# Cross-attention of a decoder layer: half of the probability tiles turned by VectorE in 32x32 squares and placed by DMA through DRAM

## The reference

```
q = (x @ Wq + bq), k = (ctx @ Wk + bk), v = (ctx @ Wv + bv)   split into 16 heads of 64
att = softmax(q * (1 / sqrt(8)) @ k.T)                        512 x 512 per batch and head
out = concat(att @ v) @ Wo + bo
x = layernorm(x + out)
```

## Time and profile before

| | us |
|---|---|
| runs shown, median of 3 (least, most) | 1960.04 (1959.64, 1960.54) |
| profiled execution, its own time | 1960.26 |
| its span, first to last instruction | 1958.4 |
| mean granted TensorE clock, share of full speed | 0.999 |
| cross-attention, roughly | 360 to 1740 |

### The profile page before, as it was taken

The page is one execution under the profiler, slowest core; times in us unless marked ns, Lnnn a source line. Parts: engine busy times, 40 slices in busy tenths (PEclk is TensorE's granted clock), DMA queues, the critical chain, the costliest instruction groups (busy, mean ns, idle before and its releaser), DMA issues.

```text
span 1958.4 us, 29643 instructions
## 1 busy us (share of the span) xinstructions
PE 1941.7 (99%) x9856; PEld 1632.4 (83%) x9856; DVE 1475.2 (75%) x3134; ACT 1149.4 (59%) x2462; POOL 729.5 (37%) x858
## 2 busy tenths in 40 slices
PE   8999999999999999999999999999999999999998
PEld 7888888788888888888888888888888888788887
DVE  5676666787777777777777777777777788867887
ACT  5445544676666666666766666666666667632221
POOL 2322342132343433332333333333333343527763
PEclk9999999999999999999999999999999999999999
DMA  5777778863556536364553726355462636321221
GB/s 215 274 285 280 300 280 318 277 218 106 185 171 189 186 116 195 98 192 140 184 168 101 237 65 215 107 162 172 119 193 66 194 115 218 130 87 44 86 87 65
DMA packets 112086, 334.87 MB, mean 171 GB/s; under 512 B 9152, under 2 KB 9152, under 8 KB 107200
## 3 DMA queue, kind: packets, MB, share of 16 engines
q1 hardware_dynamic: 111936, 332.98, 51.2%
HBM read 211.31 MB, written 88.08 MB: 153 GB/s over the span
## 4 chain that ended last, share of the span: by engine, by line
PE 94%; DVE 2%; ACT 2%; issue 1%; DMA 0%; POOL 0%; ACTq 0%; DVEq 0%; POOLq 0%
PE a_proj L1311 17%; PE a_turned L1311 17%; PE a_score L1324 11%; PE a_av L1348 11%; PE a_proj L48 9%; PE a_proj L1335 5%; PE a_turned L1335 5%; PE a_proj L1739 4%; PE a_av L1739 4%; PE a_score L48 3%; PE a_av L48 3%; ACT c_prob L1019 1%; PE a_score L1714 1%; PE a_turned L1698 1%; PE a_turned L612 1%
## 5 line engine op out<-in xcount | busy, mean ns | idle before, releaser
L958 POOL TENSOR_SCALAR c_prob<-c_prob,all_rden 128x512 f32<-128x512 f32 x512 | 350.2, 698 | 881.8 <-DVE all_rden L1128 881.8
L1019 ACT ACTIVATE c_prob<-a_score,all_negmax 128x512 f32<-128x512 f32 x512 | 348.0, 685 | 211.6 <-DVE all_negmax L1122 208.8
L1122 DVE TENSOR_REDUCE all_negmax<-a_score 128x1 f32<-128x512 f32 x512 | 329.3, 685 | 186.4 <-PE a_score L1324 186.1
L1324 PE MATMUL a_score<-c_ks,c_qs 128*128 128x512 f32 x1024 | 277.6, 391 | 3.3 <-ACT c_prob L1019 3.0
L1348 PE MATMUL a_av<-c_pt,c_vs 128*128 128x512 f32 x1024 | 277.1, 391 | 0.0
L1324 PEld LDWEIGHTS a_score<-c_ks,c_qs 128*128 128x128 f32 x1024 | 190.5, 188 | 44.7 <-ACT c_prob L1019 5.9
L1348 PEld LDWEIGHTS a_av<-c_pt,c_vs 128*128 128x128 f32 x1024 | 192.0, 188 | 39.8
L1168 DVE TENSOR_TENSOR c_pt<-a_proj,c_pt 128x512 fp32r<-128x512 f32 x258 | 171.9, 686 | 27.0 <-ACT c_pt L1047 25.0
L1311 PE MATMUL a_proj<-all_second_buffer,c_wq 128*128 128x512 f32 x756 | 188.0, 397 | 0.0
L1311 PE MATMUL a_turned<-all_third_buffer,all_first_buffer 128*128 128x512 f32 x732 | 182.6, 398 | 0.0
L1168 DVE TENSOR_TENSOR c_pt<-a_turned,c_pt 128x512 fp32r<-128x512 f32 x254 | 169.1, 686 | 9.0 <-ACT c_pt L1047 5.3
(11 more groups left out here) (207 smaller groups left out, 3275.0 us busy)
## 6 DMA issues: line engine op xcount, KB each, us to landing
all_first_buffer<-ctxT_scratch SPq DMA_DIRECT2D x64, 512.0 KB, 7.4
c_wk<-wk_scratch SPq DMA_DIRECT2D x64, 512.0 KB, 3.8
c_wq<-wq_scratch SPq DMA_DIRECT2D x64, 512.0 KB, 6.1
all_second_buffer<-x1T_scratch SPq DMA_DIRECT2D x16, 2048.0 KB, 14.8
c_ks<-c_ks SPq DMA_DIRECT2D x128, 256.0 KB, 5.6
ctxT_scratch<-s_csp SPq DMA_DIRECT2D x8, 2048.0 KB, 7.4
c_y<-y_steps_scratch SPq DMA_DIRECT2D x16, 1024.0 KB, 6.1
y_steps_scratch<-c_y SPq DMA_DIRECT2D x15, 1024.0 KB, 10.0
```

What stands on the lines that cost most here:

```text
L958: nc.gpsimd.tensor_scalar(prob[:, n % 2, i, :], prob[:, n % 2, i, :], rden[:, n % 2, i:i + 1], 1.0, ALU.mult, ALU.mult).then_inc(p_ready, 1)
L1019: nc.scalar.activation(prob[:, n % 2, i, :], spsum[:, i % 2, :], ACT.Exp, bias=negmax[:, n % 2, i:i + 1], scale=1.0, accum_out=den[:, n % ...
L1122: nc.vector.tensor_reduce(negmax[:, n % 2, i:i + 1], spsum[:, i % 2, :], AX.X, ALU.max, negate=True).then_inc(smax, 1)
L1324: ins = nc.tensor.matmul(spsum[:, i % 2, :], qs[:, j % 2, e, i * P:(i + 1) * P], ks[:, j % 2, e, m, :], start=(m == HI), stop=(m == LO))
```

## The change

For all heads but three (the first two and the last, `WHOLE`), TensorE turns only the first two blocks of 128 keys. The other two take another way. VectorE turns `prob[:, n % 2, 256:, i]` (128 x 256) of each of the four query tiles in place, in squares of 32x32 (`flip`); SyncE stores the 128 x 1024 values of the head to DRAM (`store_flips`, 512 KB) and loads them back with four DMAs, each to 32 partitions in pieces of 512 bytes (`load_flips`), to `landing`. ScalarE casts the landed tile to its high part (`flip_hi_tile`), and GpSimd subtracts in place for the low part (`flip_lo_tile`).

So that a piece is 512 bytes long, the four query tiles lie interleaved: `prob` is [128, 2, 512 keys, 4] instead of [128, 2, 4, 512 keys], and exp, normalisation and turning step over 16 bytes; the turnings write their PSUM bank with the same step (`squares`), and `o_second` reads it so and puts the queries back in order.

The order of the work changes with it. `MIDDLE`, `FIRST` and `LAST` are new orders of the items. Values of blocks 0 and 1 come two steps after their turning, those of blocks 2 and 3 in the step 2n + 4 of head n. The context and x are loaded in two pieces per step from ScalarE's queue (`BULK`), as are the V and O weights. SyncE's order is by step (`sync_step`): after the item's weights, a store of flips in an even step, their load in the odd one, then the doubling of K. The wait on the stored y moves to step 13. The tests on GpSimd's and VectorE's passed counters share one semaphore, the ready signals of V and O weights are replaced by TensorE's direct waits, x1T is loaded in four pieces, the feed-forward weights are split two to four steps later and stored by piece, and some buffers move.

```diff
@@ cross_attention
-    TILES, STEPS, LEAD, LAG = T * HH, T * HH // 2, 4, 4
+    TILES, STEPS, LEAD = T * HH, T * HH // 2, 4
+    Q, TURNED, FLIPPED = 32, 2, 2
+    SQUARES = P // Q
...
-    NEXT = ["V0+", "K0+", "Q0+", "V1+", "V2+", "K1+", "Q1+"]
-    MIDDLE = ["V3", "K2", "Q2", "O0", "O1", "O2", "K3", "Q3", "O3"] + NEXT
-    FIRST = ["V2", "V3", "K2", "", "Q2", "", "K3", "", "Q3"]
-    NEXT_TO_FIRST = NEXT
-    LAST = ["V3", "K2", "Q2", "", "O0", "", "K3", "", "Q3", "", "O1", "", "O2", "", "O3", ""]
+    NEXT = ["V0+", "K0+", "Q0+", "V1+", "K1+", "V2+"]
+    MIDDLE = ["Q1", "K2", "Q2", "V3", "O0", "O1", "K3", "Q3", "O2", "O3"] + NEXT
+    FIRST = ["V2", "K2", "Q2", "V3", "", "", "K3", "", "Q3", ""] + NEXT
+    LAST = ["Q1", "K2", "Q2", "V3", "", "O0", "K3", "Q3", "", "O1", "", "O2", "", "O3", "", ""]
...
+    WHOLE = (0, 1, HH * GROUPS - 1)
+    def turned_in(g, step):
+        n, half = divmod(step, 2)
+        return [(g, T * n + k) for k in ((2 * half, 2 * half + 1) if HH * g + n in WHOLE else (half,))]
+    def valued_in(g, step):
+        n, half = divmod(step, 2)
+        tiles = [(n - 1, 1)] if half else [(n - 2, 2), (n - 2, 3), (n - 1, 0)]
+        return [x for x in (tile_of(g, *tile) for tile in tiles) if x]
...
+    def store_flips(g, n):
+        head = HH * g + n
+        sp.wait_ge(flipped, T * FLIPS[head])
+        wait(sp, landed[head % 2], 16 * SQUARES * (LANDINGS[head] - 1))
+        sp.dma_start(flips[head % 2], prob[:, n % 2, TURNED * P:, :].rearrange("p c i -> p (c i)")).then_inc(
+            flip_stored, 16)
+    def load_flips(g, n):
+        head = HH * g + n
+        sp.wait_ge(flip_stored, 16 * FLIPS[head])
+        wait(sp, av_mm, T * (head - 1))
+        src = flips[head % 2].rearrange("(a p) (k c n) -> c p k a n", a=SQUARES, k=FLIPPED, c=SQUARES)
+        dst = as_f32(landing[:, head % 2, :, :]).rearrange("p k (a n) -> p k a n", a=SQUARES)
+        for c in range(SQUARES):
+            sp.dma_start(dst[c * Q:(c + 1) * Q], src[c]).then_inc(landed[head % 2], 16)
...
     def norm_tile(g, t):
-        nc.gpsimd.tensor_scalar(prob[:, n % 2, i, :], prob[:, n % 2, i, :], rden[:, n % 2, i:i + 1], 1.0,
+        nc.gpsimd.tensor_scalar(prob[:, n % 2, :, i], prob[:, n % 2, :, i], rden[:, n % 2, i:i + 1], 1.0,
                                 ALU.mult, ALU.mult).then_inc(p_ready, 1)
+    def flip_lo_tile(g, n, k):
+        head = HH * g + n
+        pool.wait_ge(flip_hi, FLIPPED * (FLIPS[head] - 1) + k + 1)
+        whole = landing[:, head % 2, k, :]
+        nc.gpsimd.tensor_tensor(whole, as_f32(whole), as_f32(flip_hi_part[:, k, :]), ALU.subtract).then_inc(flip_lo, 1)
...
     def pool_group(g):
+            if step == 3 and g:
+                split_out(g - 1, PAIRS - 1)
+            if landed_head(g, step):
+                for k in range(FLIPPED):
+                    flip_lo_tile(*landed_head(g, step), k)
             for tile in ahead(g, step):
                 norm_tile(*tile)
-            if step == 1 and g:
-                split_out(g - 1, PAIRS - 1)
+            if step == 0 and g:
+                split_out(g - 1, PAIRS - 2)
...
     def exp_tile(g, t):
-        nc.scalar.activation(prob[:, n % 2, i, :], spsum[:, i % 2, :], ACT.Exp,
+        nc.scalar.activation(prob[:, n % 2, :, i], spsum[:, i % 2, :], ACT.Exp,
...
+    def flip_hi_tile(g, n, k):
+        head = HH * g + n
+        act.wait_ge(landed[head % 2], 16 * SQUARES * LANDINGS[head])
+        wait(act, av_mm, T * (head - 1) + TURNED + k + 1)
+        nc.scalar.copy(flip_hi_part[:, k, :], as_f32(landing[:, head % 2, k, :])).then_inc(flip_hi, 1)
...
     def scalar_group(g):
+            if landed_head(g, step):
+                for k in range(FLIPPED):
+                    flip_hi_tile(*landed_head(g, step), k)
+            if item and item[0] != "O":
+                proj_hi_part(item)
+            for tile in tiles:
+                exp_tile(*tile)
+            if head:
+                o_first(*head)
+            for tile in turned_in(g, step):
+                pt_hi_tile(*tile)
+            if not last:
+                for operand, k in BULK.get(step, []):
+                    if operand in "cx":
+                        (load_ctx if operand == "c" else load_x)((g + 1) % NB, k)
...
+    def flip(g, t):
+        n, i = divmod(t, T)
+        dve.wait_ge(p_ready, TILES * g + t + 1)
+        block = prob[:, n % 2, TURNED * P:, i]
+        nc.vector.transpose(block, block).then_inc(flipped, 1)
...
     def vector_group(g):
+            for tile in tiles:
+                max_tile(*tile)
+            for tile in ahead(g, step - 1):
+                if HH * tile[0] + tile[1] // T in FLIPS:
+                    flip(*tile)
+            if item and item[0] in "KQ":
+                for e in range(2):
+                    proj_lo_part(item, [e])
+                    if tiles:
+                        recip(*tiles[e])
...
     def turn(g, t):
-            ins = nc.tensor.transpose(bank_of(("T", g, t))[:, i * P:(i + 1) * P],
-                                      prob[:, n % 2, i, k * P:(k + 1) * P], ident[:, :])
+            ins = nc.tensor.transpose(squares(bank_of(("T", g, t)))[:, i], prob[:, n % 2, k * P:(k + 1) * P, i],
+                                      ident[:, :])
```

More of the change, by code:

```diff
@@ L771, in ahead, with tile_of @@
         return [] if g + h == GROUPS else [(g + h, t), (g + h, t + 1)]
[L773 to L775 removed]
+    def tile_of(g, head, k):
+        return (g, T * head + k) if head >= 0 else (g - 1, T * (head + HH) + k) if g else None
+    WHOLE = (0, 1, HH * GROUPS - 1)
+    FLIPS = {head: n + 1 for n, head in enumerate(h for h in range(HH * GROUPS) if h not in WHOLE)}
+    LANDINGS = {head: sum(h % 2 == head % 2 for h in FLIPS if h <= head) for head in FLIPS}
+    def turned_in(g, step):
[5 more added lines that the diff above has]
+        return [x for x in (tile_of(g, *tile) for tile in tiles) if x]
     users = list(PROLOGUE)
@@ new lines, in sync_step @@
+        if item and item[0] in "KQV":
+            letter, G, j = item
+            sp.wait_ge(proj_mm, made(*item))
+            if letter == "V" and j == 3 and G % NB == NB - 1:
+                if last:
+                    me.after.sync_expert()
+            n = PAIRS * G + j + 1
+            if letter in "KQ" and n < PAIRS * GROUPS:
+                pair = n // (PAIRS * NB) * PAIRS + n % PAIRS
+                if letter == "K":
+                    load_pair(wk, wkparts, pair, wk_loaded)
+                else:
+                    load_pair(wq, wqparts, pair, wq_loaded)
+            if letter == "Q" and j == 3 and last:
+                me.after.sync_shared()
@@ L920, in sync_group @@
+        if head:
+            (load_flips if step % 2 else store_flips)(*head)
+        if item and item[0] == "K":
+            double_k(item[1], item[2])
+        if item == ("O", g - 1, T - 1):
             store_y(g - 1)
+        if g and step == (STEPS - 1 if last else 13):
+            sp.wait_ge(y_stored, 16 * g)
             load_y(g)
-        if opens:
-            wait(sp, wo_mm, T * g)
-            load_half(nc, WO, woparts, h, wo_loaded)
-        if not last:
-            for j in (0, 1):
-                sp.wait_ge(proj_mm, made("K", g + 1, j))
-                load_pair(wk, wkparts, nh * PAIRS + j + 1, wk_loaded)
-                double_k(g + 1, j)
-                sp.wait_ge(proj_mm, made("Q", g + 1, j))
-                load_pair(wq, wqparts, nh * PAIRS + j + 1, wq_loaded)
@@ L1361, in tensor_group @@
             item, tiles = SCHEDULE[g][step], ahead(g, step)
-            if item is None:
-                for e in range(2):
-                    if tiles:
-                        scores(*tiles[e])
-                    values_before(g, 2 * step + e)
-                    turn(g, 2 * step + e)
-            else:
+            if item:
                 project(item)
@@ L1371, in tensor_group @@
                     scores(*tile)
-                for e in range(2):
-                    values_before(g, 2 * step + e)
-                for e in range(2):
-                    turn(g, 2 * step + e)
+            elif tiles:
+                scores(*tiles[0])
+                scores(*tiles[1])
+            for tile in valued_in(g, step):
+                values(*tile)
+            for tile in turned_in(g, step):
+                turn(*tile)
             if g == GROUPS - 1 and step >= STEPS - 2:
```

316 lines of the change are left out of this document (136 added, 180 removed).

## The result

| | us |
|---|---|
| before, median of 4 runs beside it | 1960.12 |
| after, median of 4 runs (least, most) | 2099.03 (2087.08, 2102.48) |
| ratio, 95% interval | 1.070 (1.068 to 1.071) |
| predicted | 1900 (1845 to 2025) |

The forecast had the wrong sign, and the time lies 74 us above its range. In the profile after, which is read like the earlier trace rows, the chain of waits runs through TensorE for only 41% of the span instead of 94%: it leaves it above all for the flips' store and loads (DMA, 24%).

A forecast was written before the change was run, and what follows sets the result against it. The prediction took TensorE's instruction stream in the cross-attention as the bound. From 1960.3 us it took 120 for fewer turnings and added 60 for late landings, nothing for the step: 1900 us, range 1845 to 2025.

The forecast's parts named there:

- What bounds the kernel, and the stage touched: Cross-attention, 360 to 1740 us: lasts as long as TensorE's instruction stream; the change touches little outside it.
- What goes from TensorE, -120: Turnings on TensorE: 8 fewer in 125 heads at 0.125 us, 125 us, less 5 for ten steps without projection.
- The stride, taken at zero: Exp, normalisation, turnings and VectorE's output sum at 16 bytes: no added cost; upper end 0.54 us per 128x512 operation.
- VectorE's block turning, 0.41: Four 128x256 turnings per head on VectorE: 0.41 us each, or 0.69 if the stride halves the pace.
- The transfers fit at 88%: Transfer engines: about 1.05 MB more per head makes 8.7 of 9.86 us, 88% instead of 50%.
- The allowance of 8.2 us: Flips through DRAM: data must land within 8.2 us of the store's issue; a quiet head needs 7.9.
- The late landings, +60: Flips landing late: 2 us of excess in five of eight heads, half of it counting, +60 us (0 to 110).
- SyncE's queue, taken at nothing for the weights: SyncE's queue: it waits for the turnings before doubling K, which is wanted only four steps later.
- late landings (2000): Rival at ScalarE's first wait of each even step: each microsecond over 8.2 costs 62 us; 2000 us, chance 0.17.
- the stride (2010): Rival on the 16-byte step: it halves the pace, 0.9 us per head over 125 heads; 2010 us, chance 0.20.
- What would show it wrong: Longer exp, normalisation or turnings' weight loads; landing wait in nearly every head; VectorE above 95% busy; no wait and 1840.

The follow-up runs named there:

- e3: The changed kernel with contiguous probabilities (tile after tile) and without the flips' store and loads from the third turned head on: 1888.4 us, ratio 0.963.
- e2: The changed kernel with its 16-byte step, but without the flips' store and loads from the third turned head on: 1971.7 us, ratio 1.006.
- e4: The kernel before with probabilities interleaved by four (a step of 16 bytes), nothing else changed: 1998.8 us, ratio 1.020.
- e6: The changed kernel without the bulk loads of context and x for groups 1 to 15: 1976.5 us, ratio 1.008.
- e10: The changed kernel with the eight bulk pieces of a group spread over steps 6 to 11 instead of 6 to 9: 2167.3 us, ratio 1.105.

## Why the prediction failed, step by step

The prediction added -120 (TensorE), 0 (the step) and +60 (late landings) to 1960. The runs give -72 (e3), +83 (e2 against e3) and +127 (after against e2). All three terms were off in the same direction, and the step, put at nothing, is the one that had no ground.

- **What bounds the kernel, and the stage touched**: right. All of the 136 us by which the profiled executions differ lie in the cross-attention.
- **What goes from TensorE, -120**: the sum was too large. e3's pair of steps takes 5.48 + 4.56 = 10.04 against 10.89 before: 0.85 per head, not 1.0, since a block of four turnings takes 0.56 and not half of 1.00. That is 106 us. Another 34 go where I had put 5: e3 gains 72 in all. Its fourteen middle groups give 93; its first and last group take 210 us together instead of 189, so they lose 20 where their 13 flipped heads should have given 11. I had taken only 5 off for their ten steps without a projection. Whether such steps, which leave TensorE nothing to hide the others behind, or the new order of the items makes that loss wasn't tried.
- **The stride, taken at zero**: wrong, and enough by itself to undo the gain: 83 us (e3 to e2). Its own upper ends were nearly exact: I gave 0.54 for a 128x512 operation and 0.69 for the block turning; measured are +0.50, +0.51 and 0.65. VectorE's sum of the head's output takes 0.38 more. The argument for zero ("pace of an engine that handles one element after another") was no evidence about a step that no row showed. The rival priced the chain at 50 us on its own; about 8 us of the 83 are TensorE's turnings, whose steps of 4.56 us become 4.59 for four of them (1048 turnings at 0.0075), which I had as a turning of 0.25, far too much, or as nothing. Most of the rest is the lengthening of steps 2, 4, 12 and 14 by the wait for the normalisation; in the longer steps of e4's middle groups the dearer exp and normalisation cost nothing.
- **VectorE's block turning, 0.41**: right for contiguous data, 419 ns in e3.
- **The transfers fit at 88%**: on average they do, 0.74 of the stage. What decides is the quarter of the group in which they don't. I named steps 6 to 9 for it and then spread the excess over five of eight heads.
- **The allowance of 8.2 us**: wrong, and too strict. I placed the cast of the landed tiles in the even step 2n+2; the code casts them in the odd step 2n+3 (the sentence ahead of the prediction that has `landed_head` in an even step is wrong in the same way). The timeline gives 1077.8 - 1065.5 = 12.3 us. A quiet head needs 3.0 for the store, four issues of 0.61 and 3.0 for the load, 8.4 us (medians of e6): not just in time but 4 us early, and free.
- **The late landings, +60**: right in place and mechanism, half in size: 127, of which about 96 are step 10 (6.4 us in 15 groups) and about 36 step 1, the next term. At step 10 the excess is not 2 us in most heads but 6.9 us, in the mean of 12 groups, in one head of each group; and not half of it but 6.4 reach the step. The lower clock behind the stall adds to it, and nothing later absorbs it.
- **SyncE's queue, taken at nothing for the weights**: wrong. Step 1 pays 2.4 us per group (6.95 against 4.59 in e2). SyncE's timeline shows the Q weights behind its wait for the flips' store:

```profile
643.90 0.38 SPq L898 DMA_DIRECT2D flips_scratch<-c_prob  x1
...
652.60 3.49 SPq L908 DMA_DIRECT2D c_landing<-flips_scratch  x4
656.13 0.60 SPq L877 DMA_DIRECT2D c_wq<-wq_scratch  x1
```

  TensorE wants those weights from 656.6 and gets them at 662.2. The place in the queue costs only while the store lands late, here after 8.6 us: with the same order of the queue, step 1 takes 4.9 us in e6 and 4.6 in e10. Why the store is late here, steps after the bulk, stays open. I had written of the doubling of K in that place, and not of the pair of weights, which the new order of projections wants two steps after the last one instead of three or more.
- **The rivals**: late landings (2000) and the stride (2010) were the two that happened, together: 2099 lies beyond both. I gave them 0.17 and 0.20 as if each excluded the other, so that no case held both, and the range ended at 2025, near each alone.
- **What would show it wrong** named both signs that came: the exp no longer at 684 ns, and the wait for landed tiles, though in one head of eight and not in nearly every one.

## What to carry to other kernels

Before work leaves a saturated engine for the transfer queues, count the bytes and the pieces in the busiest quarter of the loop, not over the loop, and list what the issuing queue holds behind each new wait. A layout step that no row of the trace shows is priced by its upper bound until it is measured, and against the step length that the change is to bring, not the present one: the same dearer exp was hidden in e4's middle groups, in steps of 5.5 us, and no longer in the shorter and fuller ones of e2. And where two rivals have independent causes, one case must hold both.

## What was not expected of the hardware

- A step of 8 bytes costs ScalarE and GpSimd 0.03 to 0.05 us on 0.69 and a step of 16 bytes 0.50, while the weight load takes 206 to 208 ns at either, against 140. A block of four turnings that also writes PSUM in steps of 16 bytes takes 0.58 us instead of 0.56.
- A stall of 5 us of TensorE leaves a granted clock of 0.53 of full speed in the stretch of 5 us in which it ends and 0.79 in the next; by TensorE's busy time that makes about a third of what the stalls cost.
- Beside full transfer engines, loads in pieces of 512 bytes instead of 2 to 4 KB cost 76 us in all, although their own median landing hardly differs (3.0 and 2.8 us).
- Which queue issues the bulk loads decides who is late (longest waits: flips 8.1 us, or weights and x 4.9 and 3.6), not how much is lost in all (2099 and 2100 us).
